# Second layer of a two-layer mixture-of-experts kernel: routing and dispatch by sequences, slot destinations scattered at other points

## The chip, the cores and the metric

The kernel runs on one core of a Trainium2 chip. The metric is the device time of one execution in microseconds (us). TensorE (PE) does matmuls and transposes, VectorE (DVE) and ScalarE (ACT) work on 128 partitions of on-chip memory, GpSimd (POOL) issues the indirect DMAs, and SyncE (SP) issues the plain DMAs from a queue of its own. The engines run side by side and wait for each other through counting semaphores.

## The reference, cut to what matters

x has 2 sequences of 1024 tokens with 128 values. Two layers follow each other, each a token mixer and a router with 8 experts.

```python
# layer 0
y = causal_attention(layernorm(x), 16 heads) @ WO
f = top2_experts(layernorm(x), gate, w1, w2, w3)        # silu(g) * u per expert
x1 = x + silu(f) * y
# layer 1, on xn = layernorm(x1)
phi = cumsum((xn @ W_omega.T + b) * exp(log_scale) / sqrt(t))
context = [xn cos(phi), xn sin(phi), retrieved real and imaginary parts]
h = xn + gelu(layernorm(context) @ W1.T + b1) @ W2.T + b2
# eight groups of 256 tokens, each with 64 slots for each expert
raw = softmax(xn @ router); first and second choice by argmax
p1 = cumsum(m1) - m1; p2 = cumsum(m2) - m2 + count of m1   # over the group
combine = gate * one_hot(expert) * one_hot(p < 64)
f = combine @ (wo[e] @ (gelu(w0[e] x) * (w1[e] x)))       # hidden width 688
out = x1 + silu(f) * h
```

The places p1 and p2 of a token need only the tokens ahead of it in its own group of 256, so a sequence of 1024 (four groups) can be routed without the other.

## The kernel before

The 2048 tokens are 16 tiles of 128; tiles 0 to 7 are sequence 0. The order of work is written out by hand.

The attention of layer 0 runs over 8 groups of four heads (`for k in range(NG + 1)`, with `PLANS[k]`, a list of steps that TensorE, VectorE and ScalarE all walk through). A step "exp" is one bank of scores (TensorE L1585), exponentiated by ScalarE (L692); "p1" and its like find the maxima of a later group. `MIDDLE` puts further steps after the n-th "exp" that follows layer 0's experts; there are 65 of them, the last 38 being group 7. In the kernel before these are the end of layer 0 for sequence 0 (combine, gate, finish, norm), the transposes of its normalised rows (x_turn) and their router logits (logits1, at 45). Such steps use a ring of four PSUM banks (`ring_m`, banks 3 to 6); a step is handed from TensorE to VectorE by `m_ready` and back by `m_free`. Nothing of `MIDDLE` follows step 45.

After the attention, in this order: the attention output of tiles 8 to 15 is turned (L1698) and multiplied by WO (L1704); VectorE forms x1 and its moments, ScalarE the square root (L595), VectorE the normalised rows (L800); TensorE turns them (L1434, helper `across`), ScalarE copies them (L721), TensorE forms their logits (L1716) and the omega product of all tokens (L1722). VectorE routes all 16 tiles at once: maximum and difference (L1184, L1185), ScalarE's Exp (L723), softmax and the two `first_max` (L832 to L836, L1187 to L1195); `places1` on TensorE (L1478 to L1482) counts the places with a triangular and an all-ones matrix; VectorE combines them (L1199 to L1203) and writes for each group of two tiles a one-hot block [128 tokens, 2 x 512 slots] into `oh` (L1208). `oh` holds eight tiles, so block n waits for the dispatch of block n - 4. The dispatch (L1736) multiplies rows by one-hots into a bank, and ScalarE copies it to XT1 (L727), 8 groups in all, through two banks. Then TensorE averages W1g (L1740, `wg_ps`), and the experts begin.

Layer 1 has 8 experts with 6 hidden blocks each (`HT`). Per block k: a gate product (L1757, the last block L1755) and an up product (L1760) on TensorE, Gelu on ScalarE (L733), their product on VectorE (L1362, `hidden1`, counted by `hid1_done`). The down projection of expert e - 1 (L1771, `down1`) stands after block 1 of expert e, then VectorE copies its result (L1369). Between hidden products VectorE carries layer 1's recurrence (`recurrence(e, k)`, passes over 1024 or 2048 values). PSUM has two banks each for gate and up, so TensorE's block k waits for VectorE's block k - 2.

Where each slot's result must go is computed by VectorE (L1235 to L1254) before the first hidden product: for a = 0, 1 (first and second choice) slots, then destinations, in `posn`. GpSimd scatters them in 32 indirect DMAs of 128 words to `dest1` in HBM (L553), each held until (2i - 4)/3 hidden products are done. SyncE loads them back (L519) once all have landed, after the loads of expert 3 and ahead of those of expert 4, and then GpSimd scatters the experts' results (L585). The result buffer `yb1` has four places, so result e waits for the scatters of result e - 4.

SyncE's queue is in order: `load_expert(e)` asks for w0 and w1 (L505 to L507) when the gate products of expert e - 2 are done and for wo (L510 to L513) when its down projection is.

## Time and profile before

| | |
|---|---|
| timed, three runs | 656.32, 656.56 and 656.92 us, median 656.56 |
| the profiled execution's own time | 658.66 us |
| its span, first to last instruction | 656.9 us |
| TensorE busy | 594.7 us (91%) |
| VectorE busy | 490.1 us (75%) |
| ScalarE busy | 325.3 us (50%) |
| GpSimd busy | 163.5 us (25%) |
| mean granted clock of TensorE | 0.964 of 2.4 GHz |
| HBM read and written | 42.19 and 18.85 MB, 93 GB/s over the span |

The busy shares are means over stages with different limits. Times in the rows count from the span's start. "Idle before" names what released an engine; "issue" and "remote" mean that the trace names nothing. L12 is line 12 of the kernel before.

### The profile page before, as it was taken

The page shows a single profiled execution, that of the slowest core. Times are in us where ns is not written, and L with a number is a line of the kernel's source. Part 1 is how long each engine was busy: PE and PEld are TensorE (multiplying, and loading weights), DVE is VectorE, ACT ScalarE, POOL GpSimd, SP SyncE. Part 2 cuts the span into 40 slices and gives each one's busy share as a digit, 9 for nine tenths or more (in the row PEclk, how much of TensorE's full clock was granted, in tenths as well). Part 3 has the DMA queues.
Part 4 walks back from the last instruction along what each step waited for, and adds up shares of the span by engine and source line. Part 5 has one row for each costly group of instructions (what it writes and reads, how often), then busy time and mean ns, then how long its engine had stood idle before and what let it go on. Part 6 is the DMA issues. An engine that isn't in the chain of part 4 may idle for free. (4 is left out here: it accounts for less than half of the span.)

```text
span 656.9 us, 12382 instructions
## 1 busy us (share of the span) xinstructions
PE 594.7 (91%) x4214; PEld 365.6 (56%) x4215; DVE 490.1 (75%) x1169; ACT 325.3 (50%) x581; POOL 163.5 (25%) x146
## 2 busy tenths in 40 slices
PE   1878999999999999899999998949989799999996
PEld 0523644444453545899999843426446355555654
DVE  7799889999988898455555598246898288987455
ACT  1752367575766766555555467721323352254134
POOL 2000000000143441133333300000068668843200
PEclk9877799999999999999999999987999899999999
DMA  8980606060713181211111070061012114320232
GB/s 191 239 281 22 219 16 185 19 201 3 204 38 100 36 224 25 49 49 45 48 48 40 25 197 2 2 197 61 1 44 66 22 47 120 109 81 17 69 76 64
DMA packets 53692, 57.18 MB, mean 87 GB/s; under 512 B 8651, under 2 KB 37355, under 8 KB 53595
## 3 DMA queue, kind: packets, MB, share of 16 engines
q1 hardware_dynamic: 49310, 49.73, 27.1%
q0 software_dynamic: 4320, 6.81, 3.2%
...
HBM read 42.19 MB, written 18.85 MB: 93 GB/s over the span
## 5 line engine op out<-in xcount | busy, mean ns | idle before, releaser
L692 ACT ACTIVATE arena<-banks 128x512 f32<-128x512 f32 (+1 forms) x304 | 156.2, 586 | 100.3 <-PE banks L1588 57.9
L1602 PE MATMUL banks<-arena 96*128 96x512 bf16 (+3 forms) x384 | 120.4, 343 | 5.2 <-DVE mpart L1082 2.8
L1585 PE MATMUL banks<-arena 128*128 128x512 bf16 (+3 forms) x384 | 116.8, 331 | 6.5 <-ACT arena L692 2.8
L1085 DVE TENSOR_REDUCE mpart<-banks 128x1 f32<-128x512 f32 x128 | 85.8, 684 | 9.0 <-PE banks L1602 8.4
L1082 DVE CUSTOM_DVE_ANT_0 banks<-banks,arena 128x512 f32<-128x512 f32 (+1 forms) x128 | 78.9, 636 | 9.6 <-PE banks L1602 6.6
L1523 PE MATMUL banks<-arena 128*128 128x128 f32 x624 | 76.3, 275 | 1.0 <-ACT arena L642 1.0
L1523 PEld LDWEIGHTS banks<-arena 128*128 128x128 f32 x624 | 72.8, 192 | 1.5 <-ACT arena L642 1.5
L1644 PE MATMUL banks<-arena 128*9 128x512 f32 (+3 forms) x768 | 70.8, 487 | 0.0
L733 ACT ACTIVATE arena<-banks 125x512 f32<-125x512 f32 (+2 forms) x48 | 28.5, 595 | 81.0 <-PE banks L1757 57.0
L1585 PEld LDWEIGHTS banks<-arena 128*128 128x128 bf16 x384 | 38.0, 100 | 53.9 <-issue 26.0
L543 POOL DMA_INDIRECT slots<-rows_a,posn x16 | 15.5, 967 | 194.6 <-PE banks L1585 185.0
...
L1602 PEld LDWEIGHTS banks<-arena 96*128 96x128 bf16 x384 | 38.2, 101 | 36.3 <-DVE mpart L1082 9.1
L585 POOL DMA_INDIRECT results<-arena x32 | 44.7, 1395 | 37.3 <-DVE arena L1369 24.6
L1006 DVE TENSOR_TENSOR arena<-banks,arena 128x512 f32<-128x512 f32 x39 | 27.0, 692 | 33.9 <-PE banks L1523 29.3
L1588 PE MATMUL banks<-bc 128*128 128x128 bf16 x256 | 49.8, 222 | 0.0
L553 POOL DMA_INDIRECT dest<-idt,posn x32 | 44.8, 1400 | 17.2 <-issue 8.8
L1771 PEld LDWEIGHTS banks<-arena 125*128 125x128 f32 (+2 forms) x384 | 44.1, 191 | 5.2 <-issue 5.2
L1757 PE MATMUL banks<-arena 128*125 128x512 f32 (+1 forms) x80 | 42.1, 608 | 4.9 <-issue 3.4
L1760 PE MATMUL banks<-arena 128*125 128x512 f32 (+1 forms) x80 | 42.7, 616 | 3.9 <-DVE arena L1362 3.4
L1362 DVE TENSOR_TENSOR arena<-banks,arena 125x512 f32<-125x512 f32 (+2 forms) x48 | 32.3, 690 | 18.3 <-PE banks L1760 10.1
L1771 PE MATMUL banks<-arena 125*128 125x128 f32 (+2 forms) x384 | 44.3, 275 | 1.0 <-issue 1.0
...
## 6 DMA issues: line engine op xcount, KB each, us to landing
...
```

What stands on the lines that cost most here:

```text
L553: pool.indirect_dma_start(dest1, bass.IndirectOffsetOnAxis(ap=posn[:, a, n:n + 1], axis=0), idt[:, NT * a + n:NT * a + n + 1], None).then_ ...
L585: pool.indirect_dma_start(ys[1], bass.IndirectOffsetOnAxis(ap=dest[:, 4 * e + m:4 * e + m + 1], axis=0), yb1[:, e % 4, m, :], None).then_i ...
L692: act.activation(Pr[:, r % 4, heads[0]:heads[-1] + 1, 0:n], ring_e[e % 3][:, 0:len(heads) * n].rearrange("p (j c) -> p j c", j=len(heads)) ...
L1082: ins = dve.tensor_tensor_reduce(ps[:, 0:n], ps[:, 0:n], tail_mask[:, 512 - n:512], 1.0, -BIG, ALU.add, ALU.max, part)
L1085: ins = dve.tensor_reduce(part, ps[:, 0:n], AX_X, ALU.max)
L1523: ins = pe.matmul(psE[:, c % 2, 512 * w + P * k:512 * w + P * k + P], w_now[:, c % 2, w, P * k:P * k + P], xT0[:, c % 2, :], start=True, s ...
L1585: ins = pe.matmul(ring_e[e % 3][:, at * n:at * n + n], QK[:, slot, j, 1, P * kt:P * kt + P], QK[:, slot, j, 0, q:q + n], start=True, stop= ...
L1588: ins = pe.matmul(ring_e[e % 3][:, at * n:at * n + P], upper_b, ident_b, start=False, stop=True)
L1602: ins = pe.matmul(ps[:, at * n:at * n + n], QK[0:TALL, slot, j, 0, P * i:P * i + P], QK[0:TALL, slot, j, 1, 512 * half:512 * half + n], st ...
L1644: ins = pe.matmul(O[32 * j:32 * j + DK + 1, q:512], V[:, QT * b + kt, HG * hq + j, :], Pr[:, r % 4, j, 0:512 - q], start=(kt == 0), stop=( ...
L1760: pe.matmul(psE[0:hn, k % 2, 512:1024], ew[s][1][:, TW + h0:TW + h0 + hn], XT1[:, e, :, :], start=True, stop=True).then_inc(Z["u1_ps"], 1)
L1771: ins = pe.matmul(psM[:, e % 2, P * m:P * m + P], hT1[HD[k], s, k, P * m:P * m + P], ew[s][2][HD[k], k, :], start=(k == 0), stop=(k == HT ...
```

## The change

- `MIDDLE` gets steps for sequence 0 after the logits at 45: route_max (46), route_exp and the unrelated scale (49), route_choice (50), places1 (56), route_places with the one-hot blocks of groups 0 to 3 (57), into a buffer of their own, `oh0`. Each works on 8 tiles instead of 16.
- Groups 0 to 2 are dispatched into banks 0 to 2 right after the WO product and ahead of the transposes of tiles 8 to 15, group 3 behind their logits; ScalarE copies them in the same order. Groups 4 to 7 keep their place. `places1` takes six matmuls per sequence where it took five in all.
- The mean of W1g moves behind block 1 of expert 1 and the down projection of expert 0.
- Slots and destinations move into `recurrence`: slot_of(0) after hidden product (0, 0), destination(0) after (1, 0), slot_of(1) and destination(1) after (2, 1).
- Destination scatter i waits for 6 + 5i/8 hidden products; the load of the destinations stands behind the loads of expert 5.
- iota shrinks to 64 columns in `cmp` and is loaded before layer 0's experts; pscale and rpos are loaded before the attention's end; the parts of sequence 1 are stored ahead of the load of group 1.

```diff
 EXPERTS_AT = (6, 3)
 MIDDLE = {2: [("attn_turn", 0)], 4: [("attn_turn", 1)], 7: [("attn_out", 0)], 9: [("attn_out", 1)],
           16: [("combine", 0)], 19: [("combine", 1)], 21: [("gate", 0), ("gate", 1)], 25: [("finish", 0)], 26: [("finish", 1)],
-          28: [("norm", 0)], 30: [("norm", 1)], 39: [("x_turn", 0)], 41: [("x_turn", 1)], 45: [("logits1",), ("scale",)]}
+          28: [("norm", 0)], 30: [("norm", 1)], 39: [("x_turn", 0)], 41: [("x_turn", 1)], 45: [("logits1",)], 46: [("route_max",)], 49: [("route_exp",), ("scale",)], 50: [("route_choice",)], 56: [("places1",)], 57: [("route_places",)]}
...
         oh = region(18112, 8 * 512).rearrange("p (n c) -> p n c", n=8)
-        iota = region(25280, 512)
+        oh0 = region(A2 + 8192, 8 * 512).rearrange("p (n c) -> p n c", n=8)
+        iota = cmp[:, 0:C1]
...
             store_parts(0)
+            store_parts(1)
             load_group(1)
-            store_parts(1)
...
+                    sp.wait_ge(Z["blkpos_ready"], 1)
+                    sp.dma_start(iota, bass.AP(pos_rows.tensor, 2 * S, [[0, P], [1, C1]])).then_inc(Z["ld_iota"], 16)
...
+            sp.wait_ge(Z["f_done"], 2)
+            sp.dma_start(pscale, bass.AP(pos_rows.tensor, 0, [[0, P], [1, S]])).then_inc(Z["ld_L1"], 16)
+            sp.dma_start(rpos, bass.AP(pos_rows.tensor, S, [[0, P], [1, S]])).then_inc(Z["ld_L1"], 16)
             sp.wait_ge(Z["pv_done"], NG * NS)
             sp.dma_start(WomT_sb, WomT).then_inc(Z["ld_L1"], 16)
             sp.dma_start(W1g, W1T.rearrange("(c p) o -> p c o", p=P)).then_inc(Z["ld_L1"], 16)
-            sp.wait_ge(Z["f_done"], 2)
-            sp.dma_start(pscale, bass.AP(pos_rows.tensor, 0, [[0, P], [1, S]])).then_inc(Z["ld_L1"], 16)
-            sp.dma_start(rpos, bass.AP(pos_rows.tensor, S, [[0, P], [1, S]])).then_inc(Z["ld_L1"], 16)
-            sp.dma_start(iota, bass.AP(pos_rows.tensor, 2 * S, [[0, P], [1, 512]])).then_inc(Z["ld_L1"], 16)
...
-                if e == 3:
+                if e == 5:
                     sp.wait_ge(Z["scattered"], 16 * 4 * NT)
                     sp.dma_start(dest, dest1[0:SLOTS1, :].rearrange("(p j) o -> p (j o)", p=P)).then_inc(Z["dest_in"], 16)
...
-                        if NT * a + n >= 4:
-                            pool.wait_ge(Z["hid1_done"], (2 * (NT * a + n) - 4) // 3)
+                        pool.wait_ge(Z["hid1_done"], 6 + 5 * (NT * a + n) // 8)
...
+            def route_exp(b):
+                half = rt[:, 1, QT * b:QT * b + QT, :]
+                act.wait_ge(Z["gates_d"], 2 + b)
+                act.activation(half, half, ACT.Exp).then_inc(Z["gates_exp"], 1)
+
+            def dispatched(g):
+                act.wait_ge(Z["disp_ps"], g + 1)
+                ps = banks[:, g, :] if g < G1 // 2 else psM[:, g % 2, :]
+                act.copy(XT1[:, :, g, :], ps.rearrange("p (e c) -> p e c", e=E)).then_inc(Z["disp_sb"], 1)
...
+            for g in range(3):
+                dispatched(g)
...
-            act.wait_ge(Z["gates_d"], 2)
-            act.activation(rt[:, 1, :, :], rt[:, 1, :, :], ACT.Exp).then_inc(Z["gates_exp"], 1)
-
-            for g in range(G1):
-                act.wait_ge(Z["disp_ps"], g + 1)
-                act.copy(XT1[:, :, g, :], psM[:, g % 2, :].rearrange("p (e c) -> p e c", e=E)).then_inc(Z["disp_sb"], 1)
+            route_exp(1)
+            dispatched(3)
+            for g in range(G1 // 2, G1):
+                dispatched(g)
...
+            def halves(b):
+                tiles = slice(QT * b, QT * b + QT)
+                return [t[:, tiles, :] for t in R], [t[:, tiles] for t in r_], [t[:, tiles, :] for t in chosen]
+
+            def route_max(b):
+                R, r_, _ = halves(b)
+                link(dve.tensor_reduce(r_[0], R[0], AX_X, ALU.max))
+                dve.tensor_tensor(R[1], R[0], over_experts(r_[0]), ALU.subtract).then_inc(Z["gates_d"], 1)
+
+            def route_choice(b):
+                R, r_, chosen = halves(b)
+                dve.wait_ge(Z["gates_exp"], 2 + b)
+                link(dve.tensor_reduce(r_[0], R[1], AX_X, ALU.add))
+                link(dve.reciprocal(r_[1], r_[0]))
+                link(dve.tensor_tensor(R[0], R[1], over_experts(r_[1]), ALU.mult))
+                first_max(R[0], r_[0], chosen[0], R[4], r_[4])
+                link(dve.scalar_tensor_tensor(R[1], chosen[0], 0.0, R[0], ALU.is_equal, ALU.mult))
+                first_max(R[1], r_[1], chosen[1], R[4], r_[4])
+                dve.sem_inc(Z["selb_ready"], 1)
+                link(dve.scalar_tensor_tensor(R[3], chosen[0], 0.0, chosen[1], ALU.is_equal, ALU.mult))
+
+            def route_places(b, ps, read):
+                R, _, chosen = halves(b)
+                first, second, total = (ps[:, 64 * i:64 * i + 64].rearrange("p (n e) -> p n e", e=E) for i in range(3))
+                dve.wait_ge(Z["pre_ps"], 2 + b)
+                link(dve.tensor_scalar(R[7], total, float(C1), None, ALU.min))
+                dve.scalar_tensor_tensor(R[4], first, 1.0, chosen[0], ALU.add, ALU.mult)
+                dve.tensor_copy(R[5], first)
+                link(dve.tensor_tensor(R[6], second, R[7], ALU.add))
+                dve.sem_inc(read, 1)
+                link(dve.scalar_tensor_tensor(R[10], R[6], 1.0, R[3], ALU.add, ALU.mult))
+                link(dve.tensor_tensor(R[4], R[4], R[10], ALU.add))
+
+            def one_hot(g, dst):
+                dve.tensor_tensor(dst.rearrange("p i (e c) -> p i e c", e=E),
+                                  iota.unsqueeze(1).unsqueeze(1).to_broadcast([P, 2, E, C1]),
+                                  R[4][:, 2 * g:2 * g + 2, :].unsqueeze(3).to_broadcast([P, 2, E, C1]), ALU.is_equal).then_inc(Z["oh_ready"], 1)
...
+                    elif step[0] == "route_max":
+                        dve.wait_ge(Z["m_free"], unit)
+                        route_max(0)
+                    elif step[0] == "route_choice":
+                        route_choice(0)
+                    elif step[0] == "route_places":
+                        route_places(0, unit_ready(), Z["m_free"])
+                        unit += 1
+                        dve.wait_ge(Z["ld_iota"], 16)
+                        for g in range(G1 // 2):
+                            one_hot(g, oh0[:, 2 * g:2 * g + 2, :])
...
             dve.wait_ge(Z["lg_sb"], 5)
-            link(dve.tensor_reduce(r_[0], R[0], AX_X, ALU.max))
-            dve.tensor_tensor(R[1], R[0], over_experts(r_[0]), ALU.subtract).then_inc(Z["gates_d"], 1)
-            dve.wait_ge(Z["gates_exp"], 2)
...
-            dve.wait_ge(Z["pre_ps"], 2)
-            pre = [psM[:, 1, 128 * a:128 * a + 128].rearrange("p (n e) -> p n e", e=E) for a in range(2)]
-            total = psM[:, 1, 256:384].rearrange("p (n e) -> p n e", e=E)
-            link(dve.tensor_scalar(R[7], total, float(C1), None, ALU.min))
-            dve.scalar_tensor_tensor(R[4], pre[0], 1.0, chosen[0], ALU.add, ALU.mult)
...
-            dve.wait_ge(Z["ld_L1"], 16 * 7)
-            for n in range(0, NT, 2):
-                if n >= 8:
-                    dve.wait_ge(Z["disp_ps"], n // 2 - 3)
-                dve.tensor_tensor(oh[:, n % 8:n % 8 + 2, :].rearrange("p i (e c) -> p i e c", e=E),
-                                  iota[:, 0:C1].unsqueeze(1).unsqueeze(1).to_broadcast([P, 2, E, C1]),
-                                  R[4][:, n:n + 2, :].unsqueeze(3).to_broadcast([P, 2, E, C1]), ALU.is_equal).then_inc(Z["oh_ready"], 1)
-                if n == 0:
-                    dve.tensor_copy(R[5], pre[0]).then_inc(Z["pre_sb"], 1)
-
-
+            route_max(1)
+            route_choice(1)
+            route_places(1, psM[:, 1, :], Z["pre_sb"])
+            for g in range(G1 // 2, G1):
+                one_hot(g, oh[:, 2 * g - 8:2 * g - 6, :])
+
+            dve.wait_ge(Z["ld_L1"], 16 * 6)
             dve.wait_ge(Z["el_done"], 1)
             dve.memset(vecs[:, 13:14], HALF_PI)
             link(dve.tensor_scalar(pscale, pscale, vecs[:, 12:13], None, ALU.mult))
@@ -1230,10 +1271,9 @@
...
-            dve.wait_ge(Z["oh_ready"], G1)
             slots = C[:, C_SLOT:C_SLOT + NT * E].rearrange("p (n e) -> p n e", e=E)
-            dve.wait_ge(Z["pre_sb"], 2)
-            for a in range(2):
...
+            def slot_of(a):
                 picked(r_[2 + a], chosen[a], R[5 + a], R[4])
                 link(dve.tensor_tensor(R[10], R[5 + a], slots, ALU.add))
                 picked(r_[6 + a], chosen[a], R[10], R[4])
...
+            def destination(a):
                 link(dve.tensor_tensor(r_[4], r_[6 + a], r_[2 + a], ALU.subtract))
                 link(dve.tensor_scalar(r_[5], r_[6 + a], 0.0, None, ALU.is_gt))
                 link(dve.scalar_tensor_tensor(r_[2 + a], r_[2 + a], 32.0, C[:, C_GRP:C_GRP + NT], ALU.mult, ALU.add))
...
-                if (e, k) == (0, 1):
+                if (e, k) == (0, 0):
+                    slot_of(0)
+                elif (e, k) == (1, 0):
+                    destination(0)
+                elif (e, k) == (2, 1):
+                    slot_of(1)
+                    destination(1)
+                elif (e, k) == (0, 1):
...
-            def places1(ps):
...
-                pe.matmul(ps[:, 0:256], before_b, sel_b.rearrange("p a n e -> p (a n e)"), start=True, stop=False)
-                pe.matmul(odd, ones_b, halves[:, 0, :, :], start=False, stop=True)
-                pe.matmul(ps[:, 256:384], ones_b, sel_b[:, 0, :, :].rearrange("p n e -> p (n e)"), start=True, stop=False)
-                pe.matmul(total[:, 0, :, :], ones_b, first[:, 1, :, :], start=False, stop=False)
-                pe.matmul(total[:, 1, :, :], ones_b, first[:, 0, :, :], start=False, stop=True).then_inc(Z["pre_ps"], 1)
+            def places1(b, ps):
+
+                pe.wait_ge(Z["selb_ready"], 2 + b)
...
+                pe.matmul(ps[:, 0:128].rearrange("p (a m) -> p a m", a=2), before_b, tiles.rearrange("p a n e -> p a (n e)"),
+                          start=True, stop=False)
+                for a in range(2):
+                    pe.matmul(odd[:, a, 1, :, :], ones_b, part[:, a, 0, :, :], start=False, stop=a == 1)
+                pe.matmul(ps[:, 128:192], ones_b, tiles[:, 0, :, :].rearrange("p n e -> p (n e)"), start=True, stop=False)
+                for i in range(2):
+                    ins = pe.matmul(total[:, i, :, :], ones_b, part[:, 0, 1 - i, :, :], start=False, stop=i == 1)
+                ins.then_inc(Z["pre_ps"], 1)
+
+            def dispatch(g):
+                pe.wait_ge(Z["oh_ready"], g + 1)
+                ps, source = (banks[:, g, :], oh0) if g < G1 // 2 else (psM[:, g % 2, :], oh)
+                for i in range(2):
+                    ins = pe.matmul(ps, xn[:, 2 * g + i, :], source[:, (2 * g + i) % 8, :], start=(i == 0), stop=(i == 1))
+                ins.then_inc(Z["disp_ps"], 1)
...
+                    elif step[0] == "places1":
+                        ps = unit_free()
+                        places1(0, ps)
+                        pe.wait_ge(Z["pre_ps"], 2)
+                        pe.sem_inc(Z["m_ready"], 1)
+                        unit += 1
...
+            for g in range(3):
+                dispatch(g)
             for c in range(2, 4):
...
 
+            pe.wait_ge(Z["disp_sb"], 3)
             for n in range(QT, NT):
                 if n % 4 == 0:
                     pe.wait_ge(Z["xT_sb"], 3 + n // 4)
                 ins = pe.matmul(psE[:, 0, E * (n - QT):E * (n - QT) + E], xnT[:, P * n:P * n + P], gate_sb[:, 1, 0:E], start=True, stop=True)
             ins.then_inc(Z["lg_ps"], 1)
-            pe.wait_ge(Z["ld_L1"], 16 * 7)
-            for c in (1, 2, 3, 0):
+            dispatch(3)
+            pe.wait_ge(Z["ld_L1"], 16 * 6)
+            for c in (1, 2, 0, 3):
                 if c == 0:
                     pe.wait_ge(Z["lg_sb"], 5)
+                elif c == 3:
+                    pe.wait_ge(Z["disp_sb"], 4)
                 pe.matmul(psE[:, c // 2, 512 * (c % 2):512 * (c % 2) + 512], WomT_sb, xnT[:, 512 * c:512 * c + 512],
                           start=True, stop=True).then_inc(Z["om_ps"], 1)
-            places1(psM[:, 1, :])
+            places1(1, psM[:, 1, :])
             for o in range(2):
                 for c in range(4):
                     ins = pe.matmul(psO[:, o:o + 1], W1g[:, c, P * o:P * o + P], vecs[:, 6 + c:7 + c], start=(c == 0), stop=(c == 3))
             ins.then_inc(Z["cb_ps"], 1)
-            for g in range(G1):
-                pe.wait_ge(Z["oh_ready"], g + 1)
-                if g == 1:
+            for g in range(G1 // 2, G1):
+                if g == 5:
                     pe.wait_ge(Z["pre_sb"], 2)
-                if g >= 2:
+                elif g >= 6:
                     pe.wait_ge(Z["disp_sb"], g - 1)
-                for i in range(2):
-                    ins = pe.matmul(psM[:, g % 2, :], xn[:, 2 * g + i, :], oh[:, (2 * g + i) % 8, :], start=(i == 0), stop=(i == 1))
-                ins.then_inc(Z["disp_ps"], 1)
-            pe.wait_ge(Z["wprep"], 1)
-            for c in range(4):
-                ins = pe.matmul(psO[:, 512:768], ones_d[:, :], W1g[:, c, :], start=(c == 0), stop=(c == 3))
-            ins.then_inc(Z["wg_ps"], 1)
+                dispatch(g)
             pe.wait_ge(Z["om_done"], 4)
...
+                    if (e, k) == (1, 1):
+                        pe.wait_ge(Z["wprep"], 1)
+                        for c in range(4):
+                            ins = pe.matmul(psO[:, 512:768], ones_d[:, :], W1g[:, c, :], start=(c == 0), stop=(c == 3))
+                        ins.then_inc(Z["wg_ps"], 1)
```

## Rows read from the trace of the kernel before

**Rows 1.** The chain of waits in order of time: start us, us, what

```profile
577.15 5.36 PE banks L1771 x48
```

**Rows 2.** Timeline of TensorE at the hand-over: start us, us, engine, line, operation

```profile
443.22 2.15 PE L1434 MATMUL banks<-C,rows_a 128*128 128x128 f32 x8 [7.13 <-DVE rows_a L800]
445.16 3.44 PE L1716 MATMUL banks<-gate_sb,shared 128*128 128x8 f32 x16
448.44 5.55 PE L1722 MATMUL banks<-shared,arena 128*128 128x512 f32 x8
...
457.80 15.70 PE L1736 MATMUL banks<-arena,rows_a 128*128 128x512 f32 x32 [1.13 <-DVE arena L1208]
473.33 1.89 PE L1740 MATMUL banks<-arena,ones_d 128*128 128x256 f32 x8
475.06 1.02 PE L1757 MATMUL banks<-arena 128*125 128x512 f32 x2
```

**Rows 3.** Busy time, count and granted clock by stretch, TensorE first

```profile
434.00:443.20 9.20, 2.05 (x16) 1.86 (x16) 7.25 (x31) 1.49 (x2) 0.00 (x0) 0.75 0.87 276
443.20:448.50 5.30, 5.28 (x25) 4.92 (x25) 0.99 (x4) 2.45 (x3) 0.00 (x0) 0.50 0.60 187
...
518.60:529.70 11.10, 9.59 (x14) 3.18 (x15) 7.13 (x6) 2.98 (x6) 6.84 (x5) 0.69 0.12 29
```

**Rows 4.** Timeline of VectorE through the second layer's routing

```profile
415.93 0.23 DVE L1166 COPY rt<-banks 128x64 f32<-128x64 f32 x1 [2.42 <-PE banks L1689]
...
431.57 0.26 DVE L1132 RECIPROCAL rc<-banks 128x16 f32<-128x16 f32 x1 [12.73 <-PEq L1656]
...
449.88 0.29 DVE L1187 TENSOR_REDUCE rs<-rt 128x16 f32<-128x128 f32 x1 [0.38 <-ACT rt L723]
...
456.52 1.22 DVE L1208 TENSOR_TENSOR arena<-arena,rt 128x1024 f32<-128x1024 f32 x1
...
468.60 2.73 DVE L1221 SCALAR_TENSOR_TENSOR arena<-banks,vecs,arena 128x512 f32<-128x512 f32 x4
```

**Rows 5.** Timeline of TensorE among the second layer's experts

```profile
481.14 1.12 PE L1760 MATMUL banks<-arena 128*125 128x512 f32 x2 [1.62 <-DVE arena L1362]
...
490.86 5.52 PE L1771 MATMUL banks<-arena 125*128 125x128 f32 x48
...
506.27 5.52 PE L1771 MATMUL banks<-arena 125*128 125x128 f32 x48
...
518.63 1.12 PE L1757 MATMUL banks<-arena 128*124 128x512 f32 x2 [3.41 <-issue]
...
529.73 5.52 PE L1771 MATMUL banks<-arena 125*128 125x128 f32 x48
...
542.35 1.12 PE L1757 MATMUL banks<-arena 128*125 128x512 f32 x2 [1.08 <-DMA arena<-in_L_ffn_w_kernel_dram]
```

**Rows 6.** Waits, 506 to 531 us: who waited, for whom, us, times, longest

```profile
DVE arena L1369 <- remote: 7.7, 1, 7.7
```

**Rows 7.** Timeline of GpSimd, scatters of destinations and then of results

```profile
481.75 2.89 POOL L553 DMA_INDIRECT dest<-idt,posn  x1 [0.30 <-issue]
...
505.94 0.96 POOL L553 DMA_INDIRECT dest<-idt,posn  x1 [0.30 <-issue]
...
540.73 1.78 POOL L585 DMA_INDIRECT results<-arena  x1 [4.22 <-DMA arena<-dest]
```

**Rows 8.** Groups by line: line, engine, operation, count, busy us, mean ns, idle

```profile
L553 POOL DMA_INDIRECT dest<-idt,posn x32 | 44.8, 1400 | 17.2 <-issue 8.8 <-DVE posn L1254 4.7 <-DVE arena L1362 3.7
...
L727 ACT COPY arena<-banks 128x512 f32<-128x512 f32 x8 | 4.7, 586 | 19.6 <-PE banks L1736 19.6
```

**Rows 9.** List of waits of the queue on SyncE, whole span

```profile
SPq L519 <- DMA dest<-idt,posn: 18.4, 1, 18.4
```

**Rows 10.** Timeline of VectorE: the fifth expert's result is copied

```profile
569.56 0.69 DVE L1369 COPY arena<-banks 128x512 f32<-128x512 f32 x1
```

**Rows 11.** Timeline of the queue on SyncE near the kernel's start

```profile
49.52 20.81 SPq L470 DMA_DIRECT2D arena<-arena  x6
```

37 lines of the change are left out of this document (14 added, 23 removed).

## The prediction

> **What bounds the kernel now.** I read the clock and span first, then the chain of waits, then the timelines of TensorE and VectorE from 430 us on. The chain shows what ends last: from 574 us to 650 it is matmuls of TensorE one behind the other, the experts' [rows 1] among them. So a microsecond taken from TensorE's way between the end of the attention (430 us) and the last expert is a microsecond of the kernel. Three places on that way are not matmuls at full rate.
>
> The hand-over from the attention to the experts: TensorE is idle for 7.13 us until the normalised rows come, then turns them, forms the router's logits and the omega product, and dispatches the eight groups in 15.70 us, with the mean of the first layer's weights behind it; the first expert starts at 475.06 [rows 2]. The granted clock averages 0.75 over 434 to 443.2 and over 443.2 to 448.5 it is 0.50, the 1.2 GHz level [rows 3]. VectorE meanwhile routes all sixteen tiles at once: 6.6 us from its first reduction after the exponential to its first one-hot row block, and it had been idle for 12.73 us before 431.57 [rows 4].
>
> The experts: the down projections of experts 0 and 1 begin 15.41 us apart (490.86 and 506.27), but the next begins 23.46 us on, at 529.73 [rows 5]. Between them TensorE is idle for 3.41 us with no releaser named, VectorE waits 7.7 us for a signal put down to nothing in the trace [rows 6], and the clock averages 0.69 in 518.6 to 529.7 [rows 3]. That is 8.05 us over the regular period. And the fifth expert starts 1.08 us late, for its weights [rows 5], because the queue on SyncE stood 18.4 us before the load of the destinations, waiting for the scatters [rows 9].
>
> **The change part by part.**
>
> (a) Routing of sequence 0 moves into the last attention group. VectorE: 17 instructions of choice, 6 of places, at the 0.23 us of a 64-wide one and some 0.03 between, 6.0 us; four one-hot blocks at 1.22, 4.9 us; 10.9 us into the 12.73 us hole [rows 4]. The turn of the attention's outputs that stands in that hole waits up to 4 us for them, and TensorE's ring of four banks lets it go on. On TensorE six small matmuls and two waits come between the last scores; if the choices are late, it waits. I take 0; the ends are 0 and the whole choice, 14 x 0.26 = 3.6 us. A gain is excluded, nothing is removed there. ScalarE's exponential of 64 values goes between those of the scores, where ScalarE waits now and then; VectorE was idle for 0.38 us over the whole one [rows 4], and has that time in the hole: 0.
>
> (b) Three dispatches go into the idle stretch. 32 matmuls took 15.70 us, so twelve take 5.9 us of the 7.13 [rows 2]; hidden, and it keeps the engine working up to 1.2 us before the rows come. ScalarE's three copies, 0.59 each [rows 8], run while VectorE writes the normalised rows; the logits wait for them at no cost.
>
> (c) Turning and logits then start from a clock of 2.4 GHz. I take half of the gain that this could bring: the logits end at 447.3, not 448.6 (-1.3). The ends are 0 and all 5.3 us of the stretch at double rate (-2.65).
>
> (d) The fourth dispatch (four matmuls) and the eight omega matmuls follow. Those eight took 5.55 us [rows 2], 0.69 each, so twelve end at 447.3 + 8.3 = 455.6. The choice of sequence 1 is done by 452 (it starts 1.3 us earlier and is narrower), so the places now wait for TensorE, a new wait of this change: places at 456.0, first one-hot block done by 458.8, where the first dispatch was at 457.80: +1.0.
>
> (e) Only four dispatches remain. At 2.4 GHz a 512-wide matmul takes twice the 1.73/8 = 0.22 us between 473.33 and 475.06, 0.43 [rows 2]. 16 x 0.43 = 6.9 us; what 15.70 us has over 32 x 0.43 is 1.9 us, at the lower clock, and I keep all of it: 8.8, to 467.6. The copy that was hidden under the weights' mean is bare now, 0.6 [rows 8]: experts at 468.2. VectorE's four one-hot blocks, its pass over pscale and the 2.73 us for omega [rows 4] are over by 466.5, just under it. Hand-over: 475.06 - 468.2 = -6.9 (ends -5 and -9.5).
>
> (f) The mean of the first layer's weights, 1.73 us [rows 2], moves behind the down projection of expert 0, where TensorE bounds: +1.7. Its wait is for weights scaled long before. The two passes that computed slots and destinations (26 small instructions) no longer hold the first hidden product: the 1.62 us stall at 481.14 goes [rows 5], but slot_of(0), eight instructions and some 2.6 us, now stands between hidden products 0 and 1. From 475.06 to 490.86 TensorE needed 15 x 0.86 = 12.9 us and was late by 2.9; stepping through the new order I get 2.1 late, at products 4 of expert 0 and 0 of expert 1: -0.8. The second slot_of and destination (4.3 us) stand under a 5.4 us down projection: 0. Net +0.9 (ends 0 and +3).
>
> (g) SyncE: the destination load stands behind the loads of experts 4 and 5, so expert 4's weights are early: -1.1 [rows 5]. What was queued behind the wait is now experts 6 and 7, which have a whole period of slack. The results' scatters, which began at 540.73 [rows 7], begin some 16 us later in the kernel's own order; the fifth result copy (569.56 [rows 10]) needs the first result's four scatters done, which leaves about nothing: 16 + 7 + 2 us later than 541 is 566 to 570. I put +0.5 (ends 0 and +2).
>
> (h) The scatters themselves. Spaced at 8 to every 5 hidden products and started 7 us later, they can't run through a down projection any more. In the trace eleven of them ran without a gap from 505.94 [rows 7] to 519.5, one each 1.26 us, and the 8.05 us loss lies in that stretch and in no other. That is a coincidence in one trace and not a cause shown. The loss is in each timed run if the profile's is, since the timed median is only 2.1 us below the profiled time. I take it as gone: -8.05 (ends 0 and -8.05).
>
> The Trainium skill speaks against placing scatters there. The scatters took 0.96 us alone and up to 2.89 [rows 7] beside VectorE, 1.40 in the mean [rows 8]. By "SBUF — State Buffer", section "SBUF: two separate sides", descriptors written by GpSimd wait while VectorE holds the port pair that they share, and this change pushes the scatters deeper among VectorE's long passes. The trace agrees in kind; the sum would be the third rival's.
>
> (i) Near the start the second batch of parts is stored before the second group is loaded. Both are issued before the queue's next entry at 49.52 [rows 11], and the same bytes move: 0, ends -1 and +1. The pscale and rpos loads move ahead of the wait for the attention's end, where nothing is queued behind them; iota shrinks to 64 columns: 0.
>
> Sum: -6.9 + 0.9 - 1.1 + 0.5 - 8.05 = -14.65 us, on the profiled execution 658.66 - 14.65 = 644.0. The profiled execution stands 2.1 us over the timed median, 656.56; taken from that, 641.9.
>
> **The rivals.**
> 1. The loss at the third expert stays, because it hangs on something else than the scatters (ScalarE's two long passes and table loads stand there as well, and stay). For: 18 of the 32 scatters still run in that stretch. Against: they were gapless there only. 656.56 - 6.6 = 650.0.
> 2. The clock holds 2.4 GHz through logits, fourth dispatch and omega. For: the idle stretch is filled. Against: the logits are 8 wide and 1 to 2 us of waits remain. Logits 1.3 us and the twelve matmuls 3.1 us shorter, of which VectorE's chain gives back 1.3: -3.1, to 638.8. "TensorE: Matmul & The Clock Gate", Part 1, of the Trainium skill says that the default state is the throttled one and that activity releases it. By that rule this rival is the rule's own result for a filled gap.
> 3. Slower: the scatters become the bound. They start near 481 in the new time; expert 6's weights must be asked for by 554, and they are queued behind the destination load, which waits for all 32. The weights are late from a pitch of (554 - 481)/32 = 2.3 us per scatter, the kernel is slower than before from (554 + 14.7 - 481)/32 = 2.75. At 2.89 + 0.30 us [rows 7] the last scatter ends at 583, a 29 us stall: 656.56 + 14 = 671. Against: the mean is 1.40 and 0.54 of idle [rows 8].
> 4. Sequence 0's routing is late in the attention and TensorE waits the whole choice: 3.6 us more, 645.5.
>
> **How the numbers follow.** Forecast 0.47, rival 1 0.27, rival 2 0.12, rival 3 0.06, rival 4 0.08. The range from 638.0 to 651.0 holds all but rival 3 and the outer ends of (e) and (f). 0.2% (1.3 us) is what a measurement here can tell from no change; all but rival 3 are beyond it on the faster side, and I leave 0.03 for several outer ends at once: faster 0.91, same 0.03, slower 0.06.
>
> **What would show it.** (b): dispatch matmuls on TensorE right behind the attention's output product, and a clock above 0.75 in the 9 us after it. (d): TensorE, not VectorE, named before the places. (e): some 33 us from the attention's last output product (436) to the first expert, 468, where it was 39. (f): no 1.6 us stall at the third product of expert 0. (g): no wait for weights at expert 4; no wait of VectorE at the fifth result. (h): every expert's period at 15.4 us and no clock fall in them. The prediction is wrong if an expert's period is still 23 us (then it is 650), or if SyncE's wait for scatters lasts over 10 us.

## The result, and the profile after

The changed kernel takes 651.70 us in the median of six runs (649.86 to 654.16), the kernel before 656.95 in six runs beside them (656.32 to 661.28): a ratio of 0.9918, 95% interval 0.9889 to 0.9946. That is 5 us faster, where 15 were forecast, and outside the range of 638.0 to 651.0. On another occasion the ratio was 0.9895 (0.9852 to 0.9939).

| | before | after |
|---|---|---|
| profiled execution, us | 658.66 | 654.16 |
| its span, us | 656.9 | 652.4 |
| TensorE busy, us | 594.7 | 595.0 |
| VectorE busy, us | 490.1 | 493.3 |
| mean granted clock of TensorE | 0.964 | 0.966 |

From the start of the last down projection to the end both take 49.8 us. From the attention's output product to that start the changed kernel needs 166.13 us where the kernel before needed 173.05; of these 6.92 us, 2.42 are lost ahead of the output product, which leaves the 4.5 us by which the spans differ. The timeline of TensorE says where the gain and the losses stand. First the hand-over, beside [rows 2] (columns: start us, us, engine, line, operation, and in brackets the idle time and who ended it):

```profile
436.45 2.05 PE L1768 MATMUL banks<-arena 128*128 128x128 f32 x16 [0.73 <-ACT arena L730]
438.33 5.32 PE L1539 MATMUL banks<-arena,rows_a 128*128 128x512 f32 x12
445.63 0.66 PE L1482 MATMUL banks<-C,rows_a 128*128 128x128 f32 x4 [1.98 <-DVE rows_a L813]
...
447.15 3.23 PE L1783 MATMUL banks<-gate_sb,shared 128*128 128x8 f32 x16
450.23 3.76 PE L1539 MATMUL banks<-arena,rows_a 128*128 128x512 f32 x4
453.78 3.80 PE L1792 MATMUL banks<-shared,arena 128*128 128x512 f32 x8
...
460.56 8.83 PE L1539 MATMUL banks<-arena,rows_a 128*128 128x512 f32 x16 [1.02 <-DVE arena L1113]
470.15 1.09 PE L1820 MATMUL banks<-arena 128*125 128x512 f32 x2 [0.77 <-ACT arena L685]
```

L1768 is the attention's output product, which was L1704 and began at 434.03. Three dispatches (L1539, 12 matmuls) stand in the idle stretch, and of its 7.13 us 1.98 are left. From the output product to the first expert it took 41.03 us before (475.06 - 434.03) and takes 33.70 now. Busy time and granted clock in that stretch and the next (columns: us, then busy time and count of TensorE, its weight loads, VectorE, ScalarE and GpSimd, then the clock):

```profile
436.40:445.60 9.20, 7.20 (x28) 3.98 (x28) 7.24 (x31) 2.94 (x5) 0.00 (x0) 1.00 0.74 219
445.60:450.20 4.60, 4.20 (x24) 3.96 (x25) 1.00 (x4) 2.46 (x3) 0.00 (x0) 0.69 0.24 66
```

The clock that averaged 0.75 and 0.50 [rows 3] is 1.00 and 0.69.

Then the experts, TensorE again, beside [rows 5]: L1834 is the down projection (L1771 before).

```profile
484.97 5.52 PE L1834 MATMUL banks<-arena 125*128 125x128 f32 x48
490.33 1.89 PE L1854 MATMUL banks<-arena,ones_d 128*128 128x256 f32 x8
...
502.11 5.52 PE L1834 MATMUL banks<-arena 125*128 125x128 f32 x48
...
513.85 1.12 PE L1820 MATMUL banks<-arena 128*124 128x512 f32 x2 [2.78 <-ACT arena L746]
...
520.77 5.52 PE L1834 MATMUL banks<-arena 125*128 125x128 f32 x48
...
564.19 2.07 PE L1823 MATMUL banks<-arena 128*124 128x512 f32 x2 [2.94 <-DVE arena L1410]
...
572.43 5.52 PE L1834 MATMUL banks<-arena 125*128 125x128 f32 x48
```

I call the distance from one down projection to the next a period, and count it by the later one. All eight, from the first expert's start:

| period ending with the down projection of expert | before | before, second trace | after | after, second trace |
|---|---|---|---|---|
| 0 (from the first expert) | 15.80 | 15.79 | 14.82 | 14.82 |
| 1 | 15.41 | 15.41 | 17.14 | 17.14 |
| 2 | 23.46 | 22.52 | 18.66 | 18.63 |
| 3 | 16.15 | 16.75 | 15.39 | 15.39 |
| 4 | 15.28 | 15.28 | 15.28 | 15.27 |
| 5 | 15.82 | 15.82 | 20.99 | 19.70 |
| 6 | 16.61 | 16.60 | 16.66 | 16.60 |
| 7 | 13.49 | 13.49 | 13.49 | 13.50 |

Period 2 is still 3.2 us over the 15.4 that are regular, and period 5 has become 3.9 to 5.2 us longer than it was. Who waited, on VectorE at the result copies (L1417, L1369 before):

```profile
513.15 0.69 DVE L1417 COPY arena<-banks 128x512 f32<-128x512 f32 x1 [5.34 <-remote]
...
562.84 0.69 DVE L1417 COPY arena<-banks 128x512 f32<-128x512 f32 x1 [3.04 <-DMA results<-arena]
```

The first waits for the signal that the down projection of expert 1 is done. TensorE's matmuls of it are over at 502.11 + 5.52 = 507.63, so the signal is 5.5 us late. It is not the only one. TensorE's next gate product is over at 507.47 + 1.02 = 508.49, and the Gelu that waits for it starts at 513.20, 4.7 us late (ScalarE's timeline):

```profile
513.20 1.09 ACT L746 ACTIVATE arena<-banks 125x512 f32<-125x512 f32 x2 [4.82 <-remote]
```

The second copy waits until the scatters of the first result have left their place in the result buffer. GpSimd's timeline shows both causes that the experiments are about:

```profile
501.79 0.96 POOL L554 DMA_INDIRECT dest<-idt,posn  x1 [0.30 <-issue]
503.05 0.96 POOL L554 DMA_INDIRECT dest<-idt,posn  x1 [0.30 <-issue]
...
510.65 0.96 POOL L554 DMA_INDIRECT dest<-idt,posn  x1 [0.30 <-issue]
514.79 0.96 POOL L554 DMA_INDIRECT dest<-idt,posn  x1 [3.18 <-DVE arena L1410]
...
551.12 1.47 POOL L586 DMA_INDIRECT results<-arena  x1 [5.43 <-DMA arena<-dest]
...
558.75 1.90 POOL L586 DMA_INDIRECT results<-arena  x1 [0.30 <-issue]
```

From 501.79 to 510.65 eight destination scatters follow each other, 1.26 us apart, beside that down projection. The results' scatters begin at 551.12, 10.4 us later than before [rows 7]. The four of the first result are issued at 551.12, 552.89, 555.22 and 556.49.

### The profile page after: what moved, and what is told of

Its sections match the earlier page's. It is cut to its first block, busy times and chain, and to the rows that moved or that the text cites. A ratio compares the mean times of both kernels' runs of the same rounds, so it can differ in the third digit from the quotient of the medians.

```text
span 652.4 us, 12425 instructions
## 1 busy us (share of the span) xinstructions
PE 595.0 (91%) x4221; PEld 366.6 (56%) x4222; DVE 493.3 (76%) x1192; ACT 325.3 (50%) x582; POOL 161.4 (25%) x146
## 4 chain that ended last, share of the span: by engine, by line
PE 63%; DVE 19%; ACT 4%; POOL 4%; issue 4%; DMA 3%; SPq 1%; another core or an unknown queue 1%; DVEq 0%; ACTq 0%; PEldq 0%; POOLq 0%
PE banks L1581 11%; PE banks L1702 8%; PE banks L1643 7%; PE banks L1660 6%; PE banks L1593 5%; PE banks L1883 4%; POOL dest L554 4%; PE banks L1834 3%; DVE banks L1135 3%; DVE mpart L1138 3%; PE banks L1823 3%; PE banks L1820 2%; PE banks L1539 2%; ACT arena L703 2%; DVE mpart L1133 1%
## 5 line engine op out<-in xcount | busy, mean ns | idle before, releaser
L565 POOL DMA_INDIRECT results<-arena x39 | 37.8, 968 | 89.3 <-DVE arena L1029 89.3
L586 POOL DMA_INDIRECT results<-arena x32 | 42.1, 1317 | 26.2 <-DVE arena L1417 11.9
L1834 PEld LDWEIGHTS banks<-arena 125*128 125x128 f32 (+2 forms) x384 | 44.1, 191 | 5.2 <-issue 5.2
L1834 PE MATMUL banks<-arena 125*128 125x128 f32 (+2 forms) x384 | 44.3, 275 | 1.0 <-issue 1.0
```

The source lines that it names most:

```text
L1834: ins = pe.matmul(psM[:, e % 2, P * m:P * m + P], hT1[HD[k], s, k, P * m:P * m + P], ew[s][2][HD[k], k, :], start=(k == 0), stop=(k == HT ...
```

## The experiments

Two theories for period 2. **S**: the row of scatters that runs without a gap beside the down projection holds TensorE's signal up. **P**: something else at that place does it (ScalarE's sine and absolute value passes with two table loads stand there), or chance. The names in the expectations are those of the runs. "In a row" below counts scatters 1.27 us or less apart from the start of the down projection on; the expectations partly counted one or a few more.

**The iota load.** SyncE asks for iota behind the slot blocks of layer 0's experts.

```diff
-                    sp.wait_ge(Z["blkpos_ready"], 1)
-                    sp.dma_start(iota, bass.AP(pos_rows.tensor, 2 * S, [[0, P], [1, C1]])).then_inc(Z["ld_iota"], 16)
                     first_blocks()
                     later_blocks()
+                    sp.dma_start(iota, bass.AP(pos_rows.tensor, 2 * S, [[0, P], [1, C1]])).then_inc(Z["ld_iota"], 16)
```

> The changed kernel with one thing moved: SyncE asks for iota behind the slot blocks of layer 0's experts instead of ahead of the first. In the trace of the changed kernel TensorE waits 1.48 us for its first block (0.89 before the change) and its clock falls for 3.4 us there; by the end of those experts it is 1.70 us later than in the kernel before, against 0.66 us on entering them. Theory A (the iota request, 0.5 us of SyncE's queue, delays the first block and with it the clock): the extra 1.70 us goes, median about 1.7 us under the changed kernel's 651.7, so 650.0. Rival (the clock dip and the wait are chance of one execution): nothing changes, 651.7.

Measured: 646.46 us, ratio 0.9815 (0.9784 to 0.9846). TensorE's wait before the first block, by its timeline, in the kernel before:

```profile
263.73 0.30 PE L1507 MATMUL banks<-C,arena 128*128 128x128 f32 x1 [0.89 <-issue]
```

In the next run (b_copy_later), which has the load where the change puts it:

```profile
263.33 0.33 PE L1565 MATMUL banks<-C,arena 128*128 128x128 f32 x1 [1.19 <-DMA arena<-slots]
```

And with the load moved:

```profile
262.48 0.30 PE L1564 MATMUL banks<-C,arena 128*128 128x128 f32 x1 [0.89 <-issue]
```

So the load costs 0.3 us in place of the nothing that I wrote. The other 1.4 of the 1.7 us were a fall of the clock in one execution (1.48 us of wait, then matmuls at half rate); the changed kernel's second trace has 1.19 and no fall. The rest of this run's gain can't be put down to the edit: its period 2 was 15.40 us, on a chip where TensorE's signals were on time in this and the next three kernels, and the changed kernel itself was not run there.

**The fifth result copied later.**

```diff
-                    if k == 1 and e:
+                    if e and k == (1 if e < 5 else 4):
                         result1(e - 1)
```

> The changed kernel with the copies of the results of experts 4, 5 and 6 behind hidden product 4 of the next expert, not 1. In the changed kernel VectorE waits 3.04 us before the fifth result copy (562.84 us) for the scatters of the first result, TensorE then waits 2.94 us for hidden products and its clock halves for 6.8 us; the period of that expert is 20.99 us where it was 15.82. Theory B (the whole 5.2 us come from this wait for a place in the result buffer): period back to 15.4 to 15.8, median 651.7 - 5.2 = 646.5. Rival (the scatters themselves or VectorE's long passes hold TensorE there): period stays at 20 us or more, median 651 to 652.

Measured: 644.71 us, ratio 0.9774 (0.9735 to 0.9813). Period 5 is 15.80; periods 6 and 7 grew by 0.6 each. Beside the run above, which kept this wait (period 5 19.49) on the same chip, period 5 is 3.7 us shorter, of which periods 6 and 7 give back 1.2; the medians are 1.8 us apart. Theory B holds for period 5.

**Scatters held, and the sine passes moved**, on that same chip.

```diff
-                        pool.wait_ge(Z["hid1_done"], 6 + 5 * (NT * a + n) // 8)
+                        pool.wait_ge(Z["hid1_done"], max(6 + 5 * (NT * a + n) // 8, 16 if NT * a + n >= 8 else 0))
```

> The changed kernel, but the destination scatters from the ninth on wait for at least 16 hidden products, so none is issued under the down projection of expert 1, which starts near 502 us. Read the distance of the down projections of experts 1 and 2 (18.66 us in the changed kernel, 23.46 in the kernel before, 15.4 elsewhere) and when the signal of the first one's end arrives (5.5 us after its matmuls are recorded as done). Theory S (scatters in a row under this down projection hold TensorE's signals up): distance 15.4, signal on time. Theory P (ScalarE's sine and absolute value passes with their two table loads, or anything else at this place): distance stays at 18 to 19, signal still 4 to 6 us late. Later stages are slower by either, since the results' scatters begin some 20 us later and the result buffer has four places: 660 to 675 in all.

```diff
-                    if (e, k) == (2, 1):
+                    if (e, k) == (2, 2):
                         act.wait_ge(Z["phi_ready"], 1)
```

> The changed kernel, but ScalarE's two passes of 2048 values (sine, absolute value) stand behind the Gelu of block 2 of expert 2, not of block 1, so ScalarE is free under the down projection of expert 1. Theory P (ScalarE's passes there cause the late signal): the signal of the end of that down projection is on time, though VectorE waits for the sine 2 to 4 us later. Theory S (scatters): the signal is still 4 to 6 us late and the distance of the down projections is 19 us or more.

Measured, one execution each: 657.00 and 651.18 us, periods 2 of 15.39 and 20.32, both signals on time. Neither tells the theories apart, since the two kernels above had 15.40 and 15.39 there with the scatters and the passes in place. What they leave: the row of eight alone does not always do harm; and moving the sine costs 4.9 us by itself, for VectorE waits 5.95 us for ScalarE. The held kernel's later cost is plain: period 5 is 29.80, with a wait of 13.0 us for the result buffer.

**Chance or kernel: the two kernels once more, and the pace of the scatters exchanged.** All four ran on one chip.

> The kernel before, unchanged, for a second trace. In its first trace the distance of the down projections of experts 1 and 2 is 23.46 us where 15.4 is regular, and the signal of the first one's end arrives 4.0 us after its matmuls are recorded as done. Theory V (the late signal comes in some executions only, like the one in the changed kernel's trace that two related kernels don't show): 15.4 in this trace, time near 650. Theory K (in this kernel it comes each time): 20 to 24 us again, time 656 to 661.

> The changed kernel, unchanged, for a second trace beside the other variants on one chip. Theory V: distance of the down projections of experts 1 and 2 is 15.4 us and not 18.66, the wait at the fifth result copy stays (that period 19.5 to 21.0), span 648 to 650. Theory K: 18.7 again.

```diff
 # kernel before
-                        if NT * a + n >= 4:
-                            pool.wait_ge(Z["hid1_done"], (2 * (NT * a + n) - 4) // 3)
+                        pool.wait_ge(Z["hid1_done"], 6 + 5 * (NT * a + n) // 8)
...
-                if e == 3:
+                if e == 5:
                     sp.wait_ge(Z["scattered"], 16 * 4 * NT)
```

> The kernel before with the new pace of the destination scatters and the load of the destinations behind expert 5, and nothing else of the change. By my prediction the long period of expert 2 (23.46) becomes 15.4 and the wait for expert 4's weights goes (-1.1): 656.6 - 9.1 = 647.4. What the trace of the changed kernel adds: the results' scatters then start some 14 us later than 540.73 and the fifth result copy waits; the scatters start earlier than in the changed kernel (slots are known at 480), so this wait is 0 to 5 us: 648 to 653. Theory K' (the long period hangs on something outside pace and place of the scatters): 655 to 660.

The reverse of that diff in the changed kernel:

> The changed kernel with the old pace of the scatters and the load of the destinations behind expert 3. SyncE then waits for all 32 scatters ahead of expert 4's weights; the second sixteen can't start before their destinations (507.6 us in the changed kernel), so the scatters end near 546 as before and expert 4's weights (needed near 537) come some 10 us late; against that the wait at the fifth result copy (5.2 us) shrinks. Forecast: 655 to 660, the loss at expert 4's first product. Rival: if the long period of expert 2 is made by the old pace, it is back as well: 660 to 668.

Measured, the first in one execution: 657.86 (period 2 22.52), 651.22 (18.63), 654.33 (17.16; ratio 0.996, 0.9936 to 0.9984) and 661.89 (34.32; ratio 1.0057, 1.0025 to 1.0089). Theory V falls on this chip. The third time lies between the two ranges that I gave; by its periods the new pace took most of period 2's loss away and brought the wait for the result buffer (period 5 19.70). The old pace in the changed kernel is the strongest case, as its TensorE timeline shows:

```profile
499.91 5.52 PE L1835 MATMUL banks<-arena 125*128 125x128 f32 x48
...
515.84 2.07 PE L1821 MATMUL banks<-arena 128*124 128x512 f32 x2 [6.98 <-issue]
519.73 2.07 PE L1824 MATMUL banks<-arena 128*124 128x512 f32 x2 [1.82 <-issue]
523.77 2.08 PE L1819 MATMUL banks<-arena 128*128 128x512 f32 x2 [1.98 <-issue]
527.38 2.04 PE L1821 MATMUL banks<-arena 128*125 128x512 f32 x2 [1.53 <-ACT arena L747]
...
534.23 5.52 PE L1835 MATMUL banks<-arena 125*128 125x128 f32 x48
```

19 scatters in a row ran there, from 499.58 to 522.37. TensorE waits four times, half the clock follows, and 18.9 us are lost. Only pace and place of the load differ from the changed kernel, so the scatters do it, not the sine passes. My forecast for this run, late weights, was wrong; the rival had it.

**The row taken out of the kernel before.** Pace as it was, the 14th scatter and later held, load behind expert 5.

```diff
-                            pool.wait_ge(Z["hid1_done"], (2 * (NT * a + n) - 4) // 3)
+                            pool.wait_ge(Z["hid1_done"], max((2 * (NT * a + n) - 4) // 3, 16 if NT * a + n >= 13 else 0))
```

> The kernel before with its own pace of the destination scatters, but the 14th and later wait for at least 16 hidden products, so none is issued under the down projection of expert 1; the load of the destinations stands behind expert 5, so that the later scatters hold no weights up. In the kernel before some 11 scatters run in a row there and the period is 23.46 and 22.52 us; with the new pace 9 in a row and 17.16; in the changed kernel with the old pace 23 in a row and 34.32. Theory S (the length of this row of scatters sets the loss): period 15.4, the wait at the fifth result copy some 4 us, 657 - 8 - 1 + 4 = 652. Rival (the loss belongs to the place, ScalarE's sine pass and table loads, or a chance): period 19 us or more, 655 to 660.

Measured: 655.79 us, ratio 0.9947 (0.992 to 0.9974). Period 2 is 15.39: all 8 us are gone with nothing changed at the place but the scatters. Period 5 is 22.14, 6.3 us over what it was, so most of the gain is given back at the result buffer. The time is 3.8 us over theory S's 652 and lies in the rival's range; it is the period that tells the two apart.

**In the changed kernel, two repairs and then three.** The first repair is the iota load's, as above. The fifth copy now stands behind hidden product (6, 0); the third repair is the hold.

```diff
-                    if k == 1 and e:
+                    if k == 1 and e and e != 5:
                         result1(e - 1)
+                    elif (e, k) == (6, 0):
+                        result1(4)
```

> The changed kernel with iota asked for behind the slot blocks, and the copy of the fifth result behind hidden product 0 of expert 6 instead of product 1 of expert 5. Destination scatters as in the changed kernel: 9 in a row under the down projection of expert 1. Period of expert 5 15.8 instead of 19.7 to 21.0; period of expert 2 15.4 or 18.6 (both were seen). 651.5 - 4.3 - 0.3 = 646.9 with the long period of expert 2, 643.7 without.

> As k_two_edits, and the scatters from the tenth on wait for at least 15 hidden products, which leaves three or fewer under the down projection of expert 1. Theory S: period of expert 2 is 15.4, and the kernel is 3.2 us faster than k_two_edits where that one shows 18.6, not slower where it shows 15.4: 643.5 to 644. Against it the results' scatters begin 4 us later, which costs nothing as long as the fifth result is copied in time. Rival: period 18.6, 647.

Measured: 646.46 (period 2 19.68, period 5 15.27; ratio 0.9816, 0.9773 to 0.9859) and 648.71 (period 2 15.39, period 6 20.90; 0.9864, 0.9816 to 0.9912). In the traces the long period moved from 2 to 6: the held scatters make those of the results start at 554.29 and not 549.53, and the sixth copy waits. By the times the third repair gained nothing: its median is 2.2 us higher.

**How long may the row be, and does it need the sine beside it?** On one chip, against a control.

> k_two_edits once more, as the control of the other three on this chip: the period of expert 2 was 19.68 us there, with 9 destination scatters in a row from the start of the down projection of expert 1 on; the same scatters left it at 15.4 in two kernels on another chip. 19 to 20 again (646) or 15.4 (642).

```diff
+                        pool.wait_ge(Z["hid1_done"], max(6 + 5 * (NT * a + n) // 8, 15 if NT * a + n >= 12 else 0))
```

> As k_two_edits, but the scatters from the 13th on wait for 15 hidden products: 5 in a row under the down projection of expert 1, where 9 gave a loss of 4.3 us, 2 gave 0.0 and 23 gave 18.9. Theory S with a loss that grows from the first scatters of the row: 1 to 2 us, period near 17. Theory S with a row that does no harm until it is long: 15.4. If the length does not matter: 19 to 20.

> As k_two_edits, with ScalarE's sine and absolute value passes and their table loads behind block 2 of expert 2, so that they don't run beside the row of scatters. Where the same edit was made before, on a chip that showed no late signals, it cost 4.9 us by itself (VectorE waits for ScalarE). Theory S alone: TensorE's signal of the end of the down projection of expert 1 is as late as in the control (some 5 us), the period 20 us or more. Theory S with ScalarE's passes as a partner: the signal is on time and the period is 20.3, all of it VectorE's wait for ScalarE.

> As j_three_edits, with the copy of the sixth result behind hidden product 0 of expert 7 and that of the seventh behind product 2. In j_three_edits the period of expert 6 was 20.90 us, 4.3 over the 16.6 elsewhere, since the sixth copy waited for the scatters of the second result. Theory: periods 15.4, 15.4, 15.3, 15.3 and 16.6, span 644.8 - 4.3 = 640.5, median 642.5, faster than k_two_edits (646.5) and than both kernels of the case. Rival: the wait moves on once more, to the seventh copy or the last scatters: 645 to 647.

Measured, one execution each for the first three: the control 647.93, period 2 19.68. Five in a row: 647.72, period 2 15.40. The 4.3 us of period 2 are not in that time, for two reasons. This execution's hand-over took 34.95 us and the control's 32.12, with a granted clock of 0.53 and 0.86 behind the idle stretch; nothing was changed there, so that is chance. And 1.3 us come back behind the last down projection (51.06 us to the end, 49.76 in the control). The sine moved: 654.82, period 2 26.09, copy of the result as late as in the control; theory S alone. Copies and hold: 650.14 in the median, ratio 0.987 (0.9833 to 0.9906), over the forecast and over the rival's 645 to 647; one execution took 2047.70 us, of which I know nothing. The second down projection and the copy of its result, TensorE's and VectorE's timelines, in the kernel with five in a row:

```profile
503.41 5.52 PE L1835 MATMUL banks<-arena 125*128 125x128 f32 x48
510.40 0.69 DVE L1416 COPY arena<-banks 128x512 f32<-128x512 f32 x1 [1.21 <-PE banks L1835]
```

And in the control:

```profile
500.55 5.52 PE L1835 MATMUL banks<-arena 125*128 125x128 f32 x48
511.73 0.69 DVE L1416 COPY arena<-banks 128x512 f32<-128x512 f32 x1 [5.41 <-remote]
```

510.40 - 508.93 is 1.47 us late, with slack enough to cost nothing; 511.73 - 506.07 is 5.66. Over all kernels outside the first chip:

| scatters in a row | copy late by, us | period 2, us |
|---|---|---|
| 0 to 2 (i, j, m) | 0.0 to 0.1 | 15.39 to 15.40 |
| 5 (o, r, s) | 1.5 | 15.39 to 15.40 |
| 7 (g) | 4.0 | 17.16 |
| 8 (after, k, q; n with the sine moved) | 5.5 to 5.7 | 18.63 to 19.68 (n: 26.09) |
| 11 (before) | 4.1 | 22.52 to 23.46 |
| 19 (h) | 7.6, and three more waits | 34.32 |

The copy's delay does not grow evenly with the row, 4.1 us at 11 and 5.5 at 8, and it is not what fills the period. In the changed kernel the copy and the two Gelus behind it come free together at 513.2. In the kernel before there are more late signals: the gate products are over at 512.65 and 514.37, and the Gelus that wait for them start 5.3 and 8.0 us later (ScalarE's timeline):

```profile
517.98 0.60 ACT L733 ACTIVATE arena<-banks 125x512 f32<-125x512 f32 x1 [5.45 <-remote]
522.40 1.34 ACT L733 ACTIVATE arena<-banks 125x512 f32<-125x512 f32 x2 [3.83 <-remote]
```

The kernel m had every period regular (15.4, 15.4, 15.3, 15.3, 16.6, 13.5) and lost 8 us behind the experts. GpSimd's timeline there:

```profile
590.20 0.96 POOL L585 DMA_INDIRECT results<-arena  x1 [0.30 <-issue]
...
599.06 0.96 POOL L585 DMA_INDIRECT results<-arena  x1 [0.31 <-issue]
```

VectorE's first read behind the last sums, and TensorE's products around it:

```profile
603.04 0.26 DVE L1391 COPY rs<-banks 128x16 f32<-128x16 f32 x2 [3.58 <-remote]
```
```profile
596.04 1.04 PE L1867 MATMUL banks<-C,shared 128*128 128x128 f32 x8
...
608.75 6.75 PE L1876 MATMUL banks<-arena,ones_f 128*128 128x512 f32 x8 [4.80 <-DVE arena L1398]
```

Eight result scatters in a row, and VectorE reads at 603.04 what TensorE had done at 597.08, again six late and with no releaser named. With the copies later, the scatters had piled up at the end. It is the same picture with scatters of another kind. The kernels k and o show it too, more weakly. In o six result scatters run in a row from 594.42 on, beside the last down projection, whose matmuls are over at 600.44; the copy of its result starts at 603.02, 2.6 us late. In k the row is three long (from 594.82 on) and the copy 0.04 late. That is the 1.3 us that came back. No run was made that breaks the long row of m.

**Timed: the repaired kernel, and the three early dispatches undone in it.**

> The kernel of o_hold_from_13 again, now timed: the changed kernel with iota behind the slot blocks, the fifth result copied behind the first hidden product of expert 6, and the scatters from the 13th on held until 15 hidden products. In its trace all periods were regular, and from the first expert to the end it took 174.5 us where k_two_edits took 177.5 and the changed kernel 180.9 to 182.3. Theory S: 3 us under k_two_edits (646.5), so 643.5, and 7.5 to 8 under the changed kernel. Rival (what is removed here comes back elsewhere, as in m_copies_and_hold): 646 to 648.

```diff
-            for g in range(3):
-                dispatch(g)
             for c in range(2, 4):
                 pe.wait_ge(Z["xn1_ready"], c + 1)
...
+            for g in range(3):
+                dispatch(g)
```

(and the same for ScalarE's copies)

> As r_hold_timed, but the dispatches of groups 0 to 2 stand behind the transposes of tiles 8 to 15, and their copies behind those of the transposes, so that TensorE's idle stretch before the transposes is empty again (7.1 us) and the twelve matmuls stand on the way to the first expert. By steps (b) and (c) of the prediction: 12 x 0.43 = 5.2 us at 2.4 GHz, and up to 2 us more since the stretch behind the idle time runs at the lower clock: the granted clock in the idle stretch falls from 1.00 to about 0.75, and the kernel is 5 to 8 us slower than r_hold_timed. Rival (VectorE's chain of routing bounds there, and the matmuls hide beside it): 0 to 2 us slower.

Measured: 643.96 us, ratio 0.9794 (0.9767 to 0.9822), and 649.84, ratio 0.9873 (0.9835 to 0.991). The first beats both kernels of the case, the changed one by some 7 us of the median (b_copy_later has as good a ratio, 0.9774, but on the chip without late signals). What the hold adds to the other two repairs is not shown by times: the interval of its ratio overlaps that of k_two_edits (0.9773 to 0.9859), on another chip. By the traces it is 3 us from the first expert to the end, 174.5 for 177.5. The early dispatches are worth 5.9 us by the times; by the traces the way from the output product to the first expert is 40.53 instead of 33.72 us, 6.8. The stretch ahead of the transposes by busy time and clock, first with them:

```profile
435.00:444.20 9.20, 7.22 (x29) 4.00 (x29) 7.29 (x31) 2.89 (x5) 0.00 (x0) 1.00 0.77 214
```

Then without:

```profile
435.00:444.30 9.30, 2.05 (x16) 1.86 (x16) 7.22 (x31) 1.60 (x3) 0.00 (x0) 0.77 0.79 216
```

## Why the prediction was wrong

- **(a) routing in the attention, 0: right.** The attention ends 2.42 us later than in the first trace of before, but 2.34 of that stand before the steps of the change begin: the scores at 383 us are late by 2.34, the last ones by 2.42. Routing cost 0.08. The rest is one execution's chance, as the second trace shows: it starts the output product 0.91 earlier than before's second one (434.37 and 435.28). Rival 4 did not come about.
- **(b) to (e) the hand-over, -6.9: right.** -7.33 in the first pair of traces, -5.54 in the second (39.33 to 33.79), 6.8 in the kernel with this part undone. (c) gave 0.6 in place of 1.3 (logits end 13.78 after the output product starts, not 14.41). (d) The first dispatch behind the routing begins 24.11 us after the output product instead of 23.77: +0.3, not +1.0. (e) 8.83 us for sixteen matmuls, as written. Rival 2, the clock at 2.4 GHz right through, failed: the stretch behind the rows stands at 0.69. It fell back at the logits, after 1.98 us of idle time. How far it falls is partly chance: over all traces with this order of work the 4.6 to 4.7 us behind the idle stretch stand at 0.53 to 0.87, and the hand-over takes 34.98 us at the lower end and 32.11 at the upper, but 1.00 was seen in none. So the rule of the Trainium skill that I had weighed there ("TensorE: Matmul & The Clock Gate", Part 1) was right for the filled stretch, at 1.00, and did not carry over to what follows.
- **(f) the mean moved, the stall gone, +0.9: right.** -0.98 and +1.73, together +0.75.
- **(g), +0.5: wrong by 3.4 to 4.7.** Its first half was right: expert 4's weights are on time, -0.8 to -1.4 for -1.1. The step that failed is the sentence on the fifth result copy. It held a time counted in the new kernel ("566 to 570") against a due time read in the old one (569.56 [rows 10]). But everything ahead of that copy had been moved some 15 us forward by my own sum; in the new kernel VectorE is ready for it at 559.8. The wait ended at 562.84, earlier than I had thought, and was still a wait. Then the clock halved for some us and made 3.0 into 5.2 (3.9 in the second trace).
- **(h), -8.05: wrong by 3.3 to 4.2.** That the scatters are the cause was right, and the runs i, j, o and h show it on their chip. They are not the whole of it: on the first chip of the experiments rows of nine cost nothing. What failed was "they can't run through a down projection any more". I counted what the new waits permit and not how far GpSimd lagged behind them. GpSimd starts late, at 488.04, when the first destinations are there and seven hidden products are done. When the down projection of expert 1 begins at 502.11, twelve are done, which permits the scatters up to the 12th, and by 504.0 fourteen, which permits the 15th; GpSimd, at some 2.0 us each beside VectorE (seven from 488.04 to 501.79), is at the eighth. In the quiet time of VectorE it catches up at 1.26 us each, and the row is there again, eight long instead of eleven. Rival 1 (the loss stays, 650.0) came nearest in its number but for the wrong reason: it let the loss hang on something else than the scatters.
- **(i), 0: nearly right.** The order of the stores shows no cost: the attention's first products with V (L1644), which begin at 74.03 us in the first trace of before, begin between 73.5 and 74.6 in all traces of either order. iota was costed only where it went away; where it went to it passes layer 0's slot blocks, 0.3 us.
- **Rival 3** did not come about: the first scatter came at 488.04 and not near 481, but the pitch was 1.8 us and not 2.3, all 32 were issued by 544.74, and SyncE waited 4.0 us for them. The Trainium skill's rule ("SBUF — State Buffer", section "SBUF: two separate sides") is borne out in kind, scatters beside VectorE's passes take up to 2.94 us. Yet its consequence here is the opposite of what I had set against it: the harm lies in the quiet stretch, where nothing slows them.

The sum with what the traces show, first pair: -7.3 + 0.75 - 0.8 + 5.2 - 4.8 = -6.95 us, against which the attention's 2.4 us of chance stand: -4.5, the difference of the spans. Second pair: -0.9 - 5.5 + 0.75 - 1.4 + 3.9 - 3.9 = -7.05, with spans 7.0 apart.
